# A column plan ended 40 steps earlier, and 50 scatters spread over the steps behind it

## The chip, the cores and the metric

The kernel runs on one core of one Trainium2 chip. The metric is the device time of one execution in microseconds (us); the figure of a kernel is the median of its runs.

## The reference, cut to what matters

A graph network of four layers over N = 6250 nodes with D = 64 features and E = 206250 edges, sorted by destination. Each layer forms a message for each edge from its two ends and reduces the messages of a node to sum, sum of squares, greatest and least:

```python
msg = jnp.concatenate([h[src], h[dst]], axis=1) @ WM + bM
s = segment_sum(msg, dst); mean_sq = segment_sum(msg * msg, dst) / denom
mx = segment_max(msg, dst); mn = segment_min(msg, dst)
agg = jnp.concatenate([mean, mx, mn, std, var, s], axis=1)
hu = jnp.concatenate([h, agg, agg * amp, agg * att], axis=1) @ WU + bU
out = leaky_relu(batchnorm(hu / sqrt(n)) @ Wmix + bmix) + h
h = relu(batchnorm(out)) + h
```

In front stands a layer norm with a relu, and at the end the input x is added.

## The kernel before, in words

The nodes lie in 50 blocks of 125. Of a node's sources in one block, one is handled by a matmul with a one-hot operand; this covers the larger part of the edges. The sources left over are handled as "columns": rows of a table in device memory that are gathered one by one.

**The one-hot stage.** Each of the four layers has 13 chunks (NCH) of 482 destination nodes (CH), and each chunk goes through the 50 blocks (TILES). One block of one chunk is a *step*, so a layer has 13 x 50 = 650 steps, numbered 0 to 649 within the layer. In a step TensorE issues three matmuls (`products`, L1638) into one of five PSUM banks G and adds 1 to the semaphore `g_ready`; then it issues three more (`sums`, L1645) into a further bank. That makes six matmuls for a step. VectorE takes the running maximum of the bank (`greatest`, L1271; L1269 for the first two of a chunk) once `g_ready` says that it is full, and adds 1 to `g_used`; TensorE waits for `g_used` before it fills that bank again, so it can be five steps ahead of VectorE and no more. The one-hot operand is loaded by the SP queue (`fetch`, L448, one load for five steps, a ring of five) from `ohd`, which the first layer makes (`compare`, L1287, with loads of `vd`) and stores.

**The columns.** A plan made in Python (`COL_GROUPS`) holds 166 groups of one to three columns, 457 in all (STATIC). GpSimd gathers them (L808, one indirect DMA for each column, 128 rows) into a ring of five groups; a group may be gathered once `joined` says that the group five places ahead of it is done with and once `g_ready` has come to within 12 steps (AHEAD) of the step at which the group is due. VectorE works a group in at its due step and the two after it, with four instructions (L1324, L1325, L1328, L1333), between the running maxima. `COL_SPAN = (56, 580)` lays the due steps evenly over steps 56 to 580. Three steps after its end VectorE has a branch for columns past the plan, which no data of this case needs.

**The end row.** When the last group is joined, GpSimd writes the accumulators `accL` back to rows of `left` with 50 indirect DMAs (L836, 128 rows of 1 KB each, `RT` = 50), waits for all of them, and loads `left` in the order of nodes into `accL` with ten DMAs (L841). GpSimd executes its queue in order. The node part begins after step 649 (VectorE L1449 and what follows it) and needs the first two of these ten loads, then two more at every fifth of its 25 turns. In the last chunk ACT's queue also loads the results of the one-hot stage back (`load_dense`, L646) after the first 8, 24, 32 and 40 blocks, and SP's queue fetches on until half of that chunk.

`wait(eng, s, value)` waits for a semaphore and, where the value depends on the layer, adds 1 to a semaphore of its own.

Of the kernel before, what the change touches and what calls it, by code (L numbers as in the profile page):

```python
# [24 lines left out]
TILES = 50  # L25
# [26 lines left out]
NCH = 13  # L52
# [14 lines left out]
RT = TILES  # L67
# [40 lines left out]
COL_GROUPS = LEAD + [g for g in COL_GROUPS if g not in LEAD]  # L108
SLOT_COLS = [sum(w for _, _, w in COL_GROUPS[b::RING_G]) for b in range(RING_G)]

COL_SPAN = (56, 580)
AHEAD = 12

REST = RT * ROUND
BINS = ROUND + 4
# [36 lines left out]
def build(nc, x, src, dst, WM, bM, WU, bU, gamma_t, beta_t, Wmix, bmix, gamma_o, beta_o, out):  # L152
# [14 lines left out]
    with ExitStack() as ctx:  # L167
# [188 lines left out]
        def wait(eng, s, value):  # L356

            wait_at(eng, s, value)
            if not isinstance(value, int):
                eng.sem_inc(S["passed"])  # L360

        def wait_at(eng, s, value):

            eng.wait_ge(S[s] if isinstance(s, str) else s, value)
# [378 lines left out]
        def _(pool):  # L743
# [37 lines left out]
            with pool.Fori(0, LAYERS) as l:  # L781
# [16 lines left out]
                NG = len(COL_GROUPS)  # L798
                first, last = COL_SPAN
                fetched = 0  # L800
                for g, (r, t, w) in enumerate(COL_GROUPS):
                    b = g % RING_G
                    fetched += w
                    wait(pool, "joined", l * NG + g + 1)
                    wait(pool, "g_ready", l * (NCH * TILES) + first + fetched * (last - first) // STATIC - AHEAD)
                    for k in range(w):
# [26 lines left out]
                    pool.sem_inc(S["passed"])  # L833

                for t in range(RT):
                    nc.gpsimd.indirect_dma_start(left, bass.IndirectOffsetOnAxis(ap=lists[:, t * PAY + D:t * PAY + D + 1], axis=0),  # L836
                                                 acc3[:, t, :], None).then_inc(S["lf_sc"], 16)
                wait(pool, "lf_sc", (l + 1) * (16 * RT))
# [6 lines left out]
        def _(dve):  # L845
# [391 lines left out]
            def dense_part(l, numbers, chunks):  # L1237
# [97 lines left out]
                def columns_at(first, last):  # L1335


                    done, due = 0, {}
                    for g, (_, _, w) in enumerate(COL_GROUPS):
                        done += w  # L1340
                        k = first + done * (last - first) // STATIC
                        for part in range(3):
                            due.setdefault(k + part, []).append((g, part))
                    return due
# [38 lines left out]

                dense(0 if numbers else l * (NCH * TILES), COL_SPAN)

# [165 lines left out]
        def _(pe):  # L1551
# [56 lines left out]
            def layer(l, stored):  # L1608
# [74 lines left out]
                def columns(j):  # L1683

                    i = l * HALF + j
                    q = j % 2
                    for g, (j0, _, _) in enumerate(M_GROUPS):
                        if j == j0:
                            wait(pe, m_ld[g], l * 32 + 32)
                    if j >= 2:  # L1690
                        wait(pe, "t_used", i - 1)
                    for k, v in enumerate((MT, ST)):
                        for a in range(2):
                            nc.tensor.transpose(TPS[q][0:NP, (2 * k + a) * P:(2 * k + a + 1) * P],  # L1694
                                                v[:, (2 * j + a) * NP:(2 * j + a + 1) * NP], ident[:, :])
                    if j >= 1:
                        wait(pe, "t_used", i)
                    nc.tensor.matmul(BPS[0:NP, 0:P], hT[:, j * NP:(j + 1) * NP], W[:, W_BB:W_BB + P],  # L1698
                                     start=True, stop=True).then_inc(S["t_ps"], 1)
# [92 lines left out]
```

## Time and profile before

| | |
|---|---|
| time, median of 3 runs | 4816.18 us (4803.33 to 4818.72) |
| span of the profiled execution | 4821.6 us |
| TensorE busy with matmuls | 3895.8 us, 81% |
| VectorE busy | 3426.7 us, 71% |
| GpSimd busy | 2229.1 us, 46% |
| 200 scatters (L836) | 195.6 us |
| 1828 gathers (L808) | 1832.8 us |

The span reaches from the first to the last instruction of one execution; it is 5.4 us (0.1%) above the median of the runs. Busy times of the engines overlap each other. "Idle before" is the time in which an engine did nothing just before an instruction of the group; the name behind it is what ended the idle time by the semaphore events, and "remote" means that no instruction on record could be named for it.

### The profile page before, as it was taken

What the parts mean: (1) busy time and instruction counts of PE and PEld (TensorE: products, weight loads), DVE (VectorE), ACT (ScalarE), POOL (GpSimd) and SP (SyncE); (2) the same over time, 40 slices, a digit from 0 to 9 for tenths busy, and PEclk for the clock granted to TensorE, in tenths of its full rate; (3) what the DMA queues carried; (4) which work ended last, traced back from release to release, by engine and by line L of the source; (5) the groups of instructions that cost most, each with busy time, mean ns of one, the idle gap of its engine ahead of it and who ended that gap; (6) DMA issues with size and microseconds to landing.
All of it is one profiled execution on the core that took longest, in us unless ns stands there. A gap on an engine that the chain in (4) does not pass through costs nothing.

```text
span 4821.6 us, 69713 instructions
## 1 busy us (share of the span) xinstructions
PE 3895.8 (81%) x19240; PEld 2004.6 (42%) x19240; DVE 3426.7 (71%) x7809; ACT 508.7 (11%) x1496; POOL 2229.1 (46%) x2241
## 2 busy tenths in 40 slices
PE   0165999998688999999587999999597999899586
PEld 0022444443265444444265444444265444444255
DVE  5795888898477777777377777777367677777466
ACT  4211000000034000000034000000024000000024
POOL 6204566666500566666500556666500466666600
PEclk9987999999799999999799999999799999999898
DMA  6005888888741444444531444444441444444450
GB/s 176 9 16 146 223 228 217 229 234 212 208 155 58 139 137 136 139 136 136 155 117 55 136 132 127 146 135 131 140 151 40 130 137 140 134 136 131 133 171 28
DMA packets 302954, 667.77 MB, mean 138 GB/s; under 512 B 82191, under 2 KB 180677, under 8 KB 302435
## 3 DMA queue, kind: packets, MB, share of 16 engines
q1 hardware_dynamic: 188676, 419.32, 29.7%
q0 software_dynamic: 81280, 191.65, 15.3%
q10 hardware_dynamic: 32732, 54.15, 3.4%
q14 instruction: 208, 1.70, 0.1%
q8 instruction: 58, 0.95, 0.1%
HBM read 517.17 MB, written 151.72 MB: 139 GB/s over the span
## 4 chain that ended last, share of the span: by engine, by line
PE 58%; another core or an unknown queue 19%; DVE 10%; issue 6%; ACT 2%; POOL 2%; DMA 1%; ACTq 1%; DVEq 0%; SPq 0%; POOLq 0%
PE bank L1638 27%; PE bank L1645 24%; PE bank L1722 3%; DVE scr L1271 2%; POOL accL L766 1%; PE bank L1710 1%; DVE RE L1082 1%; POOL accL L758 1%; DVE accL L1038 1%; DMA RE<-vd 1%; DVE accL L1039 1%; PE bank L1620 1%; PE bank L1694 0%; ACT scr L690 0%
## 5 line engine op out<-in xcount | busy, mean ns | idle before, releaser
L808 POOL DMA_INDIRECT rows<-table,lists x1828 | 1832.8, 1003 | 1269.8 <-issue 645.0
L1638 PE MATMUL bank<-RE,split 126*128 126x482 bf16 x7800 | 2061.8, 374 | 346.5 <-DVE scr L1271 268.4
L1271 DVE TENSOR_TENSOR scr<-scr,bank 128x482 f32<-128x482 f32 x2496 | 1594.6, 649 | 1026.5 <-PE bank L1638 615.0
L1645 PE MATMUL bank<-RE,split 125*128 125x482 bf16 x7800 | 2058.5, 373 | 143.1 <-ACT scr L565 122.7
L1638 PEld LDWEIGHTS bank<-RE,split 126*128 126x128 bf16 x7800 | 749.8, 98 | 1272.9 <-DVE scr L1271 348.5
L1645 PEld LDWEIGHTS bank<-RE,split 125*128 125x128 bf16 x7800 | 766.8, 98 | 1016.1 <-ACT scr L565 128.9
L565 ACT COPY scr<-bank 128x482 f32<-128x482 f32 x52 | 29.1, 560 | 3704.9 <-PE bank L1645 1772.1
L1333 DVE TENSOR_TENSOR accL<-accL,rows 128x384 f32<-128x384 f32 (+2 forms) x664 | 342.8, 516 | 0.0
L1328 DVE SCALAR_TENSOR_TENSOR rows<-CNT,rows 128x384 f32<-128x384 f32 (+2 forms) x664 | 342.6, 516 | 0.0
L793 POOL MEMSET accL<- 128x3328 f32 x4 | 11.5, 2871 | 682.5 <-DVE split L1260 681.5
L836 POOL DMA_INDIRECT left<-accL,lists x200 | 195.6, 978 | 110.5 <-issue 110.5
L1324 DVE TENSOR_TENSOR accL<-accL,rows 128x192 f32<-128x192 f32 (+2 forms) x664 | 221.0, 333 | 1.7 <-issue 1.0
L1325 DVE TENSOR_TENSOR accL<-accL,rows 128x192 f32<-128x192 f32 (+2 forms) x664 | 220.7, 332 | 0.0
L1722 PE MATMUL bank<-W,rows 128*125 128x192 f32 x624 | 126.5, 340 | 39.8 <-ACT scr L690 39.8
L772 POOL DMA_INDIRECT pos_d<-accL,nid x50 | 50.1, 1002 | 230.5 <-DVE nid L1163 215.5
L1287 DVE TENSOR_SCALAR RE<-RE,col 126x2410 bf16<-126x2410 bf16 x130 | 113.2, 871 | 28.2 <-DMA RE<-vd 26.5
L1722 PE MATMUL bank<-W,RE 128*125 128x192 f32 x576 | 113.1, 332 | 20.2 <-ACT scr L690 19.3
L1722 PEld LDWEIGHTS bank<-W,rows 128*125 128x125 f32 x624 | 101.8, 193 | 47.9 <-issue 38.1
L1269 DVE COPY scr<-bank 128x482 f32<-128x482 f32 x104 | 67.0, 655 | 59.3 <-remote 28.4
L1722 PEld LDWEIGHTS bank<-W,RE 128*125 128x125 f32 x576 | 90.7, 187 | 28.0 <-issue 25.1
L1449 DVE TENSOR_TENSOR rows<-bank,accL 125x256 f32<-125x256 f32 x100 | 42.6, 426 | 77.8 <-PE bank L1698 76.1
L1710 PE MATMUL bank<-ident,aggb 125*128 125x125 f32 x600 | 83.4, 276 | 4.8 <-DVE aggb L1469 4.8
(272 smaller groups left out, 2370.6 us busy)
## 6 DMA issues: line engine op xcount, KB each, us to landing
RE<-ohd SPq DMA_DIRECT2D x395, 593.1 KB
RE<-vd SPq DMA_DIRECT2D x130, 593.1 KB
ohd<-RE SPq DMA_DIRECT2D x130, 593.1 KB
rows<-table,lists POOLq DMA_INDIRECT x1828
dense_d<-scr ACTq DMA_DIRECT2D x104, 241.0 KB
accL<-left POOLq DMA_DIRECT2D x40, 625.0 KB, 19.3
split<-dense_d ACTq DMA_DIRECT2D x16, 750.0 KB, 8.6
table<-accL SPq DMA_DIRECT2D x36, 250.0 KB
```

Of the source, the lines that this page charges most:

```text
L808: nc.gpsimd.indirect_dma_start(ring[:, b * GC + k, :], None, table, bass.IndirectOffsetOnAxis(ap=lists[:, c:c + 1], axis=0)).then_inc(col_ ...
L836: nc.gpsimd.indirect_dma_start(left, bass.IndirectOffsetOnAxis(ap=lists[:, t * PAY + D:t * PAY + D + 1], axis=0), acc3[:, t, :], None).the ...
L1271: nc.vector.tensor_tensor(accM[k % 2], accM[k % 2], G[k % RING][:, 0:CH], ALU.max).then_inc(S["g_used"], 1)
L1287: nc.vector.tensor_scalar(BK[b][0:NP + 1, :], VB[g % 2][0:NP + 1, :], answers[0:NP + 1, :], None, ALU.is_equal).then_inc(S["cmp"], 1)
L1324: nc.vector.tensor_tensor(acc[:, :, 2 * D:3 * D], acc[:, :, 2 * D:3 * D], got[:, :, 0:D], ALU.max)
L1325: nc.vector.tensor_tensor(acc[:, :, 3 * D:4 * D], acc[:, :, 3 * D:4 * D], got[:, :, 0:D], ALU.min).then_inc(S["tops"], 1)
L1328: nc.vector.scalar_tensor_tensor(got, bcast(CNT[:, t:t + w].unsqueeze(2), [P, w, 2 * D]), float(r), got, ALU.is_gt, ALU.mult).then_inc(S[" ...
L1333: nc.vector.tensor_tensor(acc[:, :, 0:2 * D], acc[:, :, 0:2 * D], got, ALU.add).then_inc(S["joined"], 1)
L1638: ins = nc.tensor.matmul(G[k % RING][:, 0:CH], split[0:NP + 1, ORDER[k], q, 0:2 * D], columns_of(k, NP + 1), start=q == 0, stop=q == 2)
L1645: ins = nc.tensor.matmul(SB[:, 0:CH], split[0:NP, ORDER[k], q, D:3 * D], columns_of(k, NP), start=k == 0 and q == 0, stop=k == TILES - 1 a ...
L1710: ins = nc.tensor.transpose(FPS[(2 * j + a) % 3][:, c * NP:(c + 1) * NP], agg[j % 2][0:NP, a, 2 * c:2 * c + 2, :], id125)
L1722: nc.tensor.matmul(u, aggT[j % 2][a][:, c * NP:(c + 1) * NP], W[:, W_U + c * 192:W_U + (c + 1) * 192], start=a == 0 and c == 0, stop=False ...
```

## The change

The plan of the columns spans steps 56 to 540, 40 steps fewer than before, with the same 457 columns in the same order. The 50 scatters of the end row each get a wait of their own on `g_ready`: the scatter of number t waits for step 546 + 3 t // 2 of the layer, thus 546, 547, 549, 550, 552 and so on to 619. Nothing else differs; VectorE's branch for columns past the plan moves with the end of the span, from step 583 to 543.

```diff
-COL_SPAN = (56, 580)
+COL_SPAN = (56, 540)
 AHEAD = 12
+SCATTER_AT = [COL_SPAN[1] + 6 + 3 * t // 2 for t in range(RT)]
...
                 for t in range(RT):
+                    wait(pool, "g_ready", l * (NCH * TILES) + SCATTER_AT[t])
                     nc.gpsimd.indirect_dma_start(left, bass.IndirectOffsetOnAxis(ap=lists[:, t * PAY + D:t * PAY + D + 1], axis=0),
                                                  acc3[:, t, :], None).then_inc(S["lf_sc"], 16)
                 wait(pool, "lf_sc", (l + 1) * (16 * RT))
```

## Rows read from the trace of the kernel before

**Rows 1.** The page's first line.

```profile
span 4821.6 us, 69713 instructions
```

**Rows 2.** The page's groups: busy us, mean ns of one | idle before, its releaser.

```profile
L808 POOL DMA_INDIRECT rows<-table,lists x1828 | 1832.8, 1003 | 1269.8 <-issue 645.0
...
L1271 DVE TENSOR_TENSOR scr<-scr,bank 128x482 f32<-128x482 f32 x2496 | 1594.6, 649 | 1026.5 <-PE bank L1638 615.0
...
L836 POOL DMA_INDIRECT left<-accL,lists x200 | 195.6, 978 | 110.5 <-issue 110.5
```

**Rows 3.** Windows, second layer: steps 10 to 44, steps 620 to 649.

```profile
core 0: us, PE busy (x) PEld busy (x) DVE busy (x) ACT busy (x) POOL busy (x), PEclk, DMA share, GB/s
1538.37:1579.98 41.61, 41.61 (x205) 19.75 (x204) 36.40 (x73) 0.00 (x0) 0.00 (x0) 1.00 0.46 150
...
2416.54:2452.03 35.49, 35.49 (x176) 16.85 (x175) 19.04 (x30) 0.00 (x0) 0.00 (x0) 1.00 0.77 242
```

**Rows 4.** Windows, steps 56 to 580: first layer, fourth layer, sum of all four.

```profile
503.45:1226.37 722.92, 667.76 (x3146) 304.20 (x3145) 617.44 (x1296) 6.62 (x11) 472.19 (x450) 0.97 0.86 224
...
3781.49:4506.61 725.12, 666.28 (x3146) 304.74 (x3144) 539.50 (x1190) 5.60 (x10) 444.99 (x450) 0.97 0.47 136
sum 2896.67, PE 2664.64 PEld 1220.04 DVE 2240.06 ACT 24.18 POOL 1805.10; mean PE 666.16 PEld 305.01 DVE 560.02 ACT 6.04 POOL 451.28
```

**Rows 5.** Windows, steps 584 to 649: first, second, fourth layer, sum of four.

```profile
1231.26:1378.20 146.94, 88.23 (x392) 39.26 (x391) 52.01 (x83) 0.56 (x1) 55.04 (x60) 0.78 0.73 225
2318.18:2452.03 133.85, 85.48 (x392) 38.39 (x391) 42.93 (x67) 0.56 (x1) 53.95 (x60) 0.80 0.62 186
...
4511.51:4646.77 135.26, 84.63 (x391) 38.34 (x390) 44.45 (x71) 0.56 (x1) 53.98 (x60) 0.79 0.60 184
sum 549.82, PE 344.04 PEld 154.43 DVE 182.37 ACT 2.24 POOL 216.94; mean PE 86.01 PEld 38.61 DVE 45.59 ACT 0.56 POOL 54.24
```

**Rows 6.** Windows inside two bursts of indirect DMAs, and behind the second.

```profile
386.48:446.19 59.71, 20.09 (x60) 6.99 (x61) 10.44 (x19) 8.76 (x18) 44.90 (x44) 0.59 0.45 132
...
2319.00:2340.00 21.00, 18.03 (x87) 8.14 (x85) 6.31 (x10) 0.00 (x0) 15.70 (x17) 1.00 0.47 153
2340.00:2384.00 44.00, 5.36 (x12) 1.30 (x12) 1.97 (x3) 0.00 (x0) 32.98 (x34) 0.51 0.34 118
...
2400.00:2440.00 40.00, 40.00 (x198) 18.98 (x197) 21.55 (x33) 0.00 (x0) 0.00 (x0) 1.00 0.95 272
```

**Rows 7.** Timeline of VectorE in that burst: start, us, instruction, idle before.

```profile
2326.42 0.66 DVE L1271 TENSOR_TENSOR scr<-scr,bank 128x482 f32<-128x482 f32 x1 [0.57 <-DVE scr L1271]
...
2355.49 0.66 DVE L1271 TENSOR_TENSOR scr<-scr,bank 128x482 f32<-128x482 f32 x1 [12.68 <-remote]
2371.59 0.66 DVE L1271 TENSOR_TENSOR scr<-scr,bank 128x482 f32<-128x482 f32 x1 [15.45 <-remote]
```

**Rows 8.** Timeline of GpSimd, second layer: the first scatter, the loads behind the last.

```profile
2319.42 1.00 POOL L836 DMA_INDIRECT left<-accL,lists  x1 [10.89 <-issue]
...
2385.08 5.26 POOL L841 DMA_DIRECT2D accL<-left  x10 [2.04 <-DMA left<-accL,lists]
```

**Rows 9.** Timelines of VectorE and GpSimd in the column stage.

```profile
1937.06 0.66 DVE L1271 TENSOR_TENSOR scr<-scr,bank 128x482 f32<-128x482 f32 x1 [5.08 <-PE bank L1638]
...
1935.42 0.94 POOL L808 DMA_INDIRECT rows<-table,lists  x1 [0.30 <-issue]
1941.53 0.94 POOL L808 DMA_INDIRECT rows<-table,lists  x1 [5.17 <-PE bank L1638]
```

**Rows 10.** Windows in the column stage, from a gather's start to another's.

```profile
2033.00:2157.90 124.90, 113.11 (x540) 51.81 (x539) 91.61 (x201) 1.12 (x2) 76.37 (x79) 0.99 0.48 137
...
2856.50:2881.00 24.50, 17.73 (x80) 7.67 (x79) 13.80 (x30) 0.00 (x0) 14.59 (x15) 0.85 0.38 112
2900.50:2918.40 17.90, 16.23 (x79) 7.36 (x78) 12.65 (x28) 0.00 (x0) 12.13 (x12) 1.00 0.40 117
```

**Rows 11.** The page's DMA issues: count, KB each, median us to landing.

```profile
accL<-left POOLq DMA_DIRECT2D x40, 625.0 KB, 19.3
```

## The prediction

> **What bounds the kernel now.** I read the page first. In its span [rows 1] TensorE is the busiest engine, and the costliest groups are the two matmul lines of the one-hot stage, the gathers and VectorE's running maximum. The scatters are a small group, 195.6 us for 200 [rows 2]; on the page they look like nothing. So I cut each layer into windows and asked what a step costs in each.
>
> An undisturbed step is the yardstick. Steps 10 to 44 of the second layer, before any gather, take 41.61 us for 34 steps, and steps 620 to 649 take 35.49 us for 29 [rows 3]. Both give 1.224 us for a step, with TensorE busy throughout. At this rate TensorE is the bound.
>
> Steps 56 to 580 carry the columns. They are 524 steps and would take 524 x 1.224 = 641.3 us; the four layers take 2896.67 us together, 724.2 each [rows 4]. The excess is 331.6 us in all, 82.9 for a layer.
>
> Steps 584 to 649 carry the scatters and the loads. They are 65 steps and would take 79.5 us, 318.2 for four layers; they take 549.8 [rows 5]. The excess is **231.6 us**, 4.8% of the time, and it is not spread out: the last 29 of these steps run at the yardstick [rows 3].
>
> The burst itself tells why. GpSimd starts scatter 1 at 2319.42 and the loads at 2385.08 [rows 8], and 2.04 us of the time between them is a wait: the 50 scatters take 63.6 us, 1.27 us each, of which 0.98 is busy [rows 2] and 0.3 a gap. In the first 21 us TensorE still issues 87 matmuls, nearly its full pace; in the next 44 us it issues 12, and the granted clock is 0.51, the lower of the two levels, after an engine that had been almost idle [rows 6]. The DMA engines are no explanation: their share is 0.34 there, and it is 0.95 in the window behind, where TensorE never pauses [rows 6]. VectorE's maximum still lasts 0.66 us but is preceded by 12.68 and 15.45 us of idleness [rows 7], although its bank's matmuls were issued long before. What comes late is the notice that a bank is full. TensorE then has no free bank and stops too. The same picture, 60 matmuls in 59.7 us, stands at the very start of the first layer, where another burst of 44 indirect DMAs runs [rows 6]; the change doesn't touch that one.
>
> The column stage shows a mild form. VectorE waits 5.08 us for TensorE's notice, and it gets it at 1937.06, just after GpSimd's row of gathers ended at 1936.4; GpSimd's own pause is 5.17 us, because it waits for the same count [rows 9]. There the disturbance ends itself: gathers hang on `g_ready`, so when notices stop, gathers stop, and the notices come through. The scatters of before hang on nothing and go on for 63.6 us.
>
> **The change part by part.**
>
> *The scatters.* From 546 to 619 there are 73 steps for 50 scatters: 73 x 1.224 / 49 = 1.82 us from one to the next, where the burst had 1.27. GpSimd's idle time between two grows from 0.3 to about 0.85 us on average. And each now waits for the count, which makes the disturbance end itself as in the column stage. What the 50 can still cost: below, nothing; above, what a gather costs, 82.9 / 450 = 0.18 us each, 9 us for a layer. Gathers come 1.6 us apart on average but in rows without a pause, the scatters never in such rows, so I take 1 us for a layer. The 50 waits and their increments on GpSimd cost its queue time in which it would be idle anyway; without that cover they would move the loads, which are not urgent (below). Behind the scatters in GpSimd's queue stand only the wait for their landing and the ten loads.
>
> *The loads.* The last scatter leaves at step 619, and the loads some 3 us later [rows 8], about 35 us before the stage's end instead of 67 us. They are 10 x 625 KB = 6.25 MB [rows 11], which takes 23 us at the 272 GB/s of rows 6, but it shares that rate with the other two queues. The first pair, all that the node part needs at its start, is at the front of its queue; the median load lands after 19.3 us [rows 11]. Its cover is thus 35 us against about 20. The later pairs have a fifth of the node part each. The row of ten issues takes 5.26 us without a pause [rows 8], in which notices may be late; TensorE can be five steps, 6.1 us, ahead. Bounds 0 and 5.3 us for a layer; I take 2.
>
> So the scatter part gives -231.6 + 4 x (1 + 2) = **-220 us**, bounds -232 and 4 x (9 + 5.3) - 232 = -174.
>
> *The columns.* The same 457 gathers and 166 groups lie in 484 steps: a gather each 1.059 steps, 1.30 us at the yardstick, where it was 1.147 steps or 1.40 us. GpSimd needs 1.25 us at least (0.94 and 0.30 [rows 9]). It had 10% to spare and now has 4%, so rows of gathers without a pause, which are what delays the notices, get longer. VectorE has room: 560 us busy of 724 [rows 4]; 40 maxima fewer at 0.65 us take 26 us off, so it is busy 534 us of a stage of about 700. In the first layer it is busy 617 us of 723, and would be 591 of 700; tight, but below. What limits the stage is then how fast gathers can go through the cycle of a long row and a pause. In before this is 724.2 / 450 = 1.61 us a gather over the whole stage, with rows that are short because the schedule isn't due yet. In the stretches of long rows it is 79 in 124.9 us (1.58), 12 in 17.9 us (1.49) and, at worst, 15 in 24.5 us (1.63) [rows 10]. I take 1.55, between best and worst: 450 x 1.55 = 697.5 us for steps 56 to 540, and then 40 steps at the yardstick, 49.0 us, are in the place of steps 540 to 580. That is 746.5 against 724.2, **+22.3 us for a layer, +89 in all**. Bounds: 1.49 gives 719.5 (-19 in all), 1.63 gives 782.5 (+233). A stage of 697.5 us for 484 steps is 1.44 us a step, 0.22 above the yardstick, where before it was 0.16 above.
>
> *The branch* for columns past the plan moves from step 583 to 543 and costs the same there.
>
> Sum: -220 + 89 = -131 us. Against the profiled span of 4821.6 that is 4691, against the median of the runs, 5.4 lower, **4685 us** (-2.7%).
>
> **Rivals.**
>
> 1. *The columns cost nothing.* Each gather keeps its excess of 0.18 us, however dense. Then only the 220 us count: 4596. For it: windows with more gathers don't look slower in steps; 12 in 17.9 us come with 79 matmuls, 1.36 us a step [rows 10]. Chance 0.09.
> 2. *The gathers keep their pace of 1.61 us.* If what delays notices works like a cap on the rate of indirect DMAs, the column stage takes its 724 us for 484 steps too, and the 40 freed steps come on top: +49 us a layer, +196. Then 4816 - 220 + 196 = 4792. For it: the four layers are alike within 1% although the first has 224 GB/s of DMA traffic and the last 136 [rows 4]. Against it: 1.49 us occurs. Chance 0.17. If it gets as bad as 1.63 everywhere the sum is +13 and the time 4829, the same as before within what can be told; 0.03.
> 3. *The loads come too late.* In the last 35 us of the stage the DMA engines move 9.5 MB at 272 GB/s; the ten loads, ACT's loads of results and the last fetches want more. If the first pair comes 15 us after the stage's end in each layer: 4685 + 60 = 4745. Against it: the pair is first in its queue. The Trainium skill, in "DMA: Bandwidth & Descriptors", section "Queues, rings and completion order", says that a DMA engine takes turns between the queues that have work, by packets; by that the loads would get at least a third of the rate, so the pair's 1.25 MB would be there in about 14 us. No row of before shows that split. Chance 0.06.
> 4. *The price is for each scatter, not for the row of them* (the other side). Divided up, the burst costs 231.6 / 200 = 1.16 us a scatter, about what one keeps GpSimd busy (0.978 us [rows 2]). If every scatter stops VectorE while it is issued, spacing gives nothing back, and the columns' price stays: 4816 + 89 = 4905. It decides as soon as more than 0.6 of that price stays with each spaced scatter. The Trainium skill, in "SBUF — State Buffer", section "Who interferes with whom", has a rule that points this way: VectorE and GpSimd share a pair of ports under an exclusive lock, the loser blocks for the whole instruction. It adds that an instruction with one operand in SBUF doesn't take part, and the maximum has one there and one in PSUM. By that lock each of 50 scatters would cost 0.97 us, near the 1.16. The rows speak against it: the first 17 scatters let 87 matmuls through and the next 34 only 12 [rows 6], the maximum isn't longer in the burst [rows 2, 7], and 450 gathers as long as a scatter cost 0.18 us each. Chance 0.05.
> 5. *The change doesn't do what it says*: GpSimd comes to the end row so late that the steps waited for are past and the scatters leave in a row again. The last group is due at 540 and the first scatter at 546, and a late GpSimd holds up the due steps too; chance 0.02, with a time near 4905.
>
> **How the numbers follow.** The likeliest case, scatters cured and columns dearer by -5 to +40 us a layer, has 0.58 and a range of its own of 4596 to 4755. A measurement of this kernel tells about 0.3%, 14 us, from no change. Faster: 0.58 + 0.09 + 0.17 + 0.06 = 0.90. Same: 0.03. Slower: 0.05 + 0.02 = 0.07. The range goes from the price-free columns to just short of rival 2, whose upper half stays out with the slower cases: 4595 to 4785.
>
> **What would show it.** In the changed profile: steps 584 to 649 in 80 to 85 us instead of 134 to 147, with TensorE's granted clock at 1.00 there; scatters with two distances, about 1.3 and 2.4 us, and idle time that ends with TensorE; no wait of VectorE over some 5 us outside the start of the first layer; the loads about 35 us before the node part and no wait of the first VectorE instruction of the node part for them. Steps 56 to 540 in about 698 us: 675 would be rival 1, 724 rival 2. The forecast is wrong if TensorE's pauses in steps 546 to 619 add up to more than 15 us a layer, or if the column stage is outside 670 to 735 us.

## The result, and the profile after

The changed kernel takes **4860.24 us** in the median of 4 runs (4852.42 to 4875.11), the kernel before 4817.45 in its 4 (4803.33 to 4822.94). The ratio is 1.0084, with a 95% interval of 1.0054 to 1.0115. So it is slower by 0.8%, a small loss, but the interval does not reach 1, where I had forecast 4685 us and a chance of 0.90 for faster. The profiled execution after has a span of 4852.7 us, 31.1 more than [rows 1], and that is the difference to explain.

The page of the changed kernel, its groups in the form of [rows 2]:

```profile
span 4852.7 us, 70113 instructions
...
L809 POOL DMA_INDIRECT rows<-table,lists x1828 | 1815.5, 993 | 1319.7 <-issue 656.4
...
L1273 DVE TENSOR_TENSOR scr<-scr,bank 128x482 f32<-128x482 f32 x2496 | 1608.0, 652 | 1048.4 <-PE bank L1640 583.1
...
L838 POOL DMA_INDIRECT left<-accL,lists x200 | 199.3, 997 | 216.6 <-PE bank L1640 168.7
```

Lines have moved: L808 is now L809, L836 is L838, L1271 is L1273, L1638 is L1640. The scatters (L838) did what was meant: GpSimd is idle for 216.6 us ahead of them instead of 110.5, and 168.7 us of that end with TensorE's count. Nothing else on the page shows where the time went, so the windows must.

Windows of the changed kernel, steps 584 to 649 in the four layers and their sum, to hold against [rows 5]:

```profile
1292.36:1403.63 111.27, 85.10 (x391) 38.97 (x390) 49.44 (x78) 0.56 (x1) 31.97 (x35) 0.86 0.89 269
2409.95:2489.50 79.55, 79.55 (x391) 37.75 (x390) 43.27 (x67) 0.56 (x1) 28.66 (x35) 1.00 0.79 229
3503.40:3582.95 79.55, 79.55 (x392) 37.75 (x391) 43.28 (x67) 0.56 (x1) 28.66 (x35) 1.00 0.79 228
4599.18:4678.73 79.55, 79.55 (x391) 37.75 (x390) 43.27 (x67) 0.56 (x1) 28.68 (x35) 1.00 0.80 224
sum 349.92, PE 323.75 PEld 152.22 DVE 179.26 ACT 2.25 POOL 117.97; mean PE 80.94 PEld 38.05 DVE 44.82 ACT 0.56 POOL 29.49
```

Three layers run at exactly the yardstick of 1.224 us for a step, with TensorE busy throughout and its granted clock at 1.00. The first layer has 31.7 us too many. In all 349.9 us stand where 549.8 stood: **-199.9 us**, where I forecast -220.

Windows of the changed kernel, steps 56 to 540, which now carry the whole plan (second and fourth layer, sum of all four), and then steps 56 to 580, the stretch of [rows 4] (fourth layer, sum):

```profile
1620.24:2356.11 735.87, 638.22 (x2906) 286.17 (x2904) 516.39 (x1150) 5.79 (x10) 441.17 (x450) 0.93 0.45 127
...
3813.06:4545.34 732.28, 642.15 (x2906) 286.15 (x2905) 515.45 (x1148) 5.04 (x9) 439.70 (x450) 0.93 0.44 128
sum 2930.61, PE 2560.36 PEld 1142.92 DVE 2136.66 ACT 22.36 POOL 1786.77; mean PE 640.09 PEld 285.73 DVE 534.16 ACT 5.59 POOL 446.69
...
3813.06:4594.29 781.23, 691.10 (x3146) 309.39 (x3144) 546.52 (x1202) 5.60 (x10) 461.97 (x473) 0.93 0.45 130
sum 3126.43, PE 2756.18 PEld 1235.77 DVE 2264.11 ACT 24.61 POOL 1877.74; mean PE 689.05 PEld 308.94 DVE 566.03 ACT 6.15 POOL 469.44
```

The plan takes 2930.6 / 4 = 732.7 us for 484 steps. Before it took 724.2 us for 524. The steps have become fewer and the time has not: 450 gathers in 732.7 us are 1.63 us each, after 1.61. Over the same steps 56 to 580 the sum grows from 2896.7 to 3126.4: **+229.8 us**, where I forecast +89. The two stretches give -199.9 + 229.8 = +29.9, and the span has grown by 31.1. All else together moved by 1.2 us.

Of the 140 us a layer that the plan's steps take over the yardstick (732.7 against 592.4), TensorE is idle for 92.6; the rest are the same matmuls taking longer, 640.1 us busy, at a granted clock of 0.93. Without the gathers (experiment 8 below) they are busy for 592.7 us at 1.00. So about a third of the loss is paid in the clock that falls with the pauses.

What a bad moment of the column stage looks like after, in the timeline of GpSimd and then of VectorE (second layer; start, us, instruction, idle time ahead and its releaser), and the window over it:

```profile
2112.16 0.94 POOL L809 DMA_INDIRECT rows<-table,lists  x1 [0.30 <-PE bank L1640]
...
2128.96 0.94 POOL L809 DMA_INDIRECT rows<-table,lists  x1 [0.30 <-issue]
2135.38 0.98 POOL L809 DMA_INDIRECT rows<-table,lists  x1 [5.47 <-DVE accL L1335]
```

```profile
2125.24 0.66 DVE L1273 TENSOR_TENSOR scr<-scr,bank 128x482 f32<-128x482 f32 x1 [3.10 <-PE bank L1640]
...
2132.28 0.66 DVE L1273 TENSOR_TENSOR scr<-scr,bank 128x482 f32<-128x482 f32 x1 [5.84 <-remote]
```

```profile
2122.00:2133.00 11.00, 4.07 (x21) 1.58 (x18) 2.05 (x6) 0.00 (x0) 6.08 (x7) 0.77 0.35 101
```

It is the cycle of [rows 9] again. GpSimd issues one gather each 1.25 to 1.57 us without a pause until 2128.96; VectorE goes on at 2132.28, 2.4 us after that last gather has ended; TensorE is busy for 4.07 of the 11 us in between. That VectorE is late, and not TensorE, shows in TensorE's own timeline (three matmuls a line):

```profile
2119.61 0.78 PE L1640 MATMUL bank<-RE,split 126*128 126x482 bf16 x3
...
2125.96 0.78 PE L1640 MATMUL bank<-RE,split 126*128 126x482 bf16 x3 [1.29 <-issue]
...
2132.99 1.39 PE L1640 MATMUL bank<-RE,split 126*128 126x482 bf16 x3 [5.64 <-DVE scr L1273]
```

Counted off from the start of the execution, one filled bank to each maximum, the maximum at 2132.28 takes the bank that was filled from 2119.61 to 2120.39. Four more banks had been filled behind it, the last from 2125.96, and then TensorE had no free one. Counted in this way over the steps 56 to 540, VectorE stands idle with its next bank already full for 140 us in the first layer and 210 to 216 in each of the others (by the ends of matmuls that the trace models); in the kernel without gathers, experiment 8, it is 2 and 35 us. GpSimd's own pause is ended here by VectorE's join (L1335), because the ring of five groups is full. Over the whole kernel the waits of gathers for joins rise from 112.1 to 234.8 us, and those for TensorE's count fall from 427.6 to 360.2: GpSimd is now behind the plan so often that the plan holds it up less, and the ring more.

### The profile page after: what moved, and what is told of

It is laid out like the page before. It is cut to its first block, busy times and chain, and to the rows that moved or that the text cites. A ratio compares the mean times of both kernels' runs of the same rounds, so it can differ in the third digit from the quotient of the medians.

```text
span 4852.7 us, 70113 instructions
## 1 busy us (share of the span) xinstructions
PE 3965.6 (82%) x19240; PEld 2014.5 (42%) x19240; DVE 3439.9 (71%) x7809; ACT 509.0 (10%) x1496; POOL 2216.5 (46%) x2241
## 4 chain that ended last, share of the span: by engine, by line
PE 53%; another core or an unknown queue 18%; DVE 13%; issue 9%; ACT 2%; DMA 2%; POOL 1%; ACTq 1%; DVEq 0%; SPq 0%
PE bank L1640 25%; PE bank L1647 22%; PE bank L1724 3%; DVE scr L1273 2%; DMA RE<-vd 1%; PE bank L1712 1%; DVE rows L1330 1%; DVE RE L1084 1%; POOL accL L767 1%; POOL accL L759 1%; DVE accL L1040 1%; DVE accL L1041 1%; DVE accL L1335 1%; PE bank L1622 1%
## 5 line engine op out<-in xcount | busy, mean ns | idle before, releaser
L809 POOL DMA_INDIRECT rows<-table,lists x1828 | 1815.5, 993 | 1319.7 <-issue 656.4
L1640 PE MATMUL bank<-RE,split 126*128 126x482 bf16 x7800 | 2097.4, 379 | 384.5 <-DVE scr L1273 292.1
L1273 DVE TENSOR_TENSOR scr<-scr,bank 128x482 f32<-128x482 f32 x2496 | 1608.0, 652 | 1048.4 <-PE bank L1640 583.1
L1647 PE MATMUL bank<-RE,split 125*128 125x482 bf16 x7800 | 2092.3, 378 | 64.0 <-ACT scr L566 37.3
L1640 PEld LDWEIGHTS bank<-RE,split 126*128 126x128 bf16 x7800 | 754.2, 99 | 1351.5 <-DVE scr L1273 389.8
L1335 DVE TENSOR_TENSOR accL<-accL,rows 128x384 f32<-128x384 f32 (+2 forms) x664 | 344.2, 518 | 0.0
L838 POOL DMA_INDIRECT left<-accL,lists x200 | 199.3, 997 | 216.6 <-PE bank L1640 168.7
L794 POOL MEMSET accL<- 128x3328 f32 x4 | 11.5, 2870 | 600.7 <-DVE split L1262 599.7
L773 POOL DMA_INDIRECT pos_d<-accL,nid x50 | 50.7, 1015 | 230.9 <-DVE nid L1165 216.0
L1271 DVE COPY scr<-bank 128x482 f32<-128x482 f32 x104 | 66.5, 656 | 30.0 <-PE bank L1640 12.5
```

Source lines behind the costliest of these rows:

```text
L809: nc.gpsimd.indirect_dma_start(ring[:, b * GC + k, :], None, table, bass.IndirectOffsetOnAxis(ap=lists[:, c:c + 1], axis=0)).then_inc(col_ ...
L1273: nc.vector.tensor_tensor(accM[k % 2], accM[k % 2], G[k % RING][:, 0:CH], ALU.max).then_inc(S["g_used"], 1)
L1335: nc.vector.tensor_tensor(acc[:, :, 0:2 * D], acc[:, :, 0:2 * D], got, ALU.add).then_inc(S["joined"], 1)
L1640: ins = nc.tensor.matmul(G[k % RING][:, 0:CH], split[0:NP + 1, ORDER[k], q, 0:2 * D], columns_of(k, NP + 1), start=q == 0, stop=q == 2)
L1647: ins = nc.tensor.matmul(SB[:, 0:CH], split[0:NP, ORDER[k], q, D:3 * D], columns_of(k, NP), start=k == 0 and q == 0, stop=k == TILES - 1 a ...
```

## The experiments

The kernel before took 4824.15 us in the median of 7 runs beside experiments 1 to 4, 4824.4 (one run) beside 5 to 8, and 4821.75 (7 runs) beside 9 to 12. Experiments 4, 5 to 8 and 12 have one run each; they are read by their windows.

### 1. The scatters' waits alone

```diff
 COL_SPAN = (56, 580)
+SCATTER_AT = [586 + t for t in range(RT)]
...
                 for t in range(RT):
+                    wait(pool, "g_ready", l * (NCH * TILES) + SCATTER_AT[t])
```

> The columns stay on steps 56 to 580; only the scatters get waits, scatter t for step 586 + t, so 586 to 635. Before, the scatters' steps 584 to 620 had an excess of 231.6 us over the yardstick of 1.224 us a step, in the changed kernel 0 us. If unbroken rows of indirect DMAs are what delays the notices, and the pace of the rows is limited to one in about 1.6 us (theory CAP), 50 scatters one step apart take 50 x 1.6 = 80 us where 49 steps take 60: an excess of about 20 us a layer, so 231.6 - 80 = 150 us less than before, about 4665. If what matters is only that the scatters hang on the count (theory SELF-ENDING), the excess is under 8 us a layer and the time about 4610, plus what the loads behind step 635, 17 us before the node part, hold that up. The column stage should take its 724 us a layer again by both.

It took 4635.41 us (4631.70 to 4646.80), ratio 0.9609 (0.9570 to 0.9649): **-189 us**. Steps 56 to 580 sum to 2891.70, as before. Windows of this kernel, steps 584 to 649, second layer and sum of four:

```profile
2281.79:2369.70 87.91, 82.25 (x392) 37.83 (x391) 40.80 (x67) 0.56 (x1) 53.93 (x60) 0.98 0.67 218
...
sum 352.25, PE 329.56 PEld 151.30 DVE 175.26 ACT 2.24 POOL 219.66; mean PE 82.39 PEld 37.83 DVE 43.81 ACT 0.56 POOL 54.91
```

The sum of [rows 5] was 549.8. The excess over 318.2 is now 34.1 us, 8.5 for a layer, with the 50 scatters 1.46 us apart in the second layer. In the changed kernel they are 1.82 us apart and the excess of the three undisturbed layers is nil. Spacing cures the burst, and how far depends on the distance. The time lies between what the two theories gave, 4665 for a limit of 1.6 us on scatters too and 4610 for none: scatters that each wait for a step went faster than the gathers ever did, at a small price. Of the gain in the windows, 12.3 us are paid back behind the stage, where VectorE waits for the loads.

### 2. The shorter plan alone

```diff
-COL_SPAN = (56, 580)
+COL_SPAN = (56, 540)
```

> The columns are put on steps 56 to 540 and the scatters get no waits: the other half of the change alone. CAP: the gathers keep their 1.60 to 1.63 us each, steps 56 to 540 take about 733 us a layer as in the changed kernel, +230 us over before for steps 56 to 580, and the burst of scatters costs about its 54 to 67 us a layer again, at step 546: about 5045. If the columns' excess came from something that the waiting scatters do (they are behind all gathers in the queue, so this is unlikely), steps 56 to 540 would take less than 700 us.

It took 5057.18 us (5052.59 to 5066.10), ratio 1.0485 (1.0443 to 1.0526): **+233 us**. Its steps 56 to 540 sum to 2943.88, 736.0 for a layer. The bursts of scatters are back in the 109 steps behind, which take 187.9 us on average and would take 133.4. The two halves add up: -189 + 233 = +44, and the whole change measured +43. That they do so this well is partly luck: experiment 1 still pays 34.1 us for its scatters and 12.3 for the loads, and the whole change pays 31.7 in the first layer's tail in their place. The sign is plain all the same. The shorter plan is the loss.

### 3. A wait for each gather

Before, the wait stands ahead of a group of up to three gathers. Here each gather has its own:

```diff
...
-                    wait(pool, "g_ready", ... + first + fetched * (last - first) // STATIC - AHEAD)
                     for k in range(w):
+                        wait(pool, "g_ready", ... + first + (fetched - w + k + 1) * (last - first) // STATIC - AHEAD)
```

> As before, but each gather waits for its own share of the schedule, 1.147 steps after the one ahead of it, where a group of up to three waited once and left in a row. If the price comes from the length of unbroken rows (theory ROWS), the rows are gone at the yardstick's pace (1.40 us from gather to gather against 1.25 needed), and the column stage's excess of 83 us a layer falls by at least a third: 4700 or less. If it is a limit on the mean pace of indirect DMAs, 1.6 us each (CAP), nothing changes within 20 us a layer: 4740 to 4900.

It took 4919.76 us (4913.97 to 4931.34), ratio 1.0200 (1.0158 to 1.0242). Steps 56 to 580, sum: 2995.03, which is 98 us more than [rows 4]. The stage takes 748.8 us a layer and the gathers come 1.66 us apart, slower than both theories had it (4700 or less, and 4740 to 4900). It does not test row length, though: I had expected the rows to be gone, and they are not. Gathers that follow each other without a pause come in rows of 5.4 on average, where the kernel before has 6.6, and rows of ten or more still hold a third of all gathers, where it was 43%. GpSimd is behind the schedule, so most of the new waits are over before it comes to them. What the length of the rows is worth stays open.

### 4. The plan over steps 56 to 640

```diff
-COL_SPAN = (56, 580)
+COL_SPAN = (56, 640)
```

> The columns are laid over steps 56 to 640, the scatters behind them without waits: read only the column stage; the scatters and loads now stand in the way of the node part, which makes the whole slower. A gather is due each 1.278 steps, 1.564 us at the yardstick. CAP: 457 gathers at 1.6 us take 731 us; steps 56 to 640 take 584 x 1.224 = 715 us without excess, so an excess of only 10 to 30 us a layer, and the pace of the gathers is 1.6 to 1.62 us for the third time. If each gather costs 0.18 us however dense (the first rival of the prediction), the excess stays at 83 us.

One run: 4581.21 us. The stage runs almost at the yardstick. The scatters now leave at the very end of the stage and behind it, and the node part waits for their rows. Timelines of this kernel, the loads on GpSimd and the first instruction of the node part on VectorE:

```profile
2341.40 3.72 POOL L841 DMA_DIRECT2D accL<-left  x7 [2.06 <-DMA left<-accL,lists]
```

```profile
2349.99 0.43 DVE L1449 TENSOR_TENSOR rows<-bank,accL 125x256 f32<-125x256 f32 x1 [66.38 <-DMA accL<-left]
```

The wait of 66.38 us is what the node part pays for a plan that ends late, and the kernel is still 5% faster. It is timed again as experiment 9.

### 5 to 8. What in a gather sets the pace

If the pace of 1.6 us is a limit, what is it a limit of? Four edits of the changed kernel, all with the plan over 56 to 540, each take one thing away. Three of them (5, 6 and 8) also clear the gathers' buffer once, ahead of the first layer, since part of it is no longer filled. Half the rows of each gather:

```diff
-  nc.gpsimd.indirect_dma_start(ring[:, b * GC + k, :], None, table, bass.IndirectOffsetOnAxis(ap=lists[:, c:c + 1], axis=0))
+  nc.gpsimd.indirect_dma_start(ring[0:64, b * GC + k, :], None, table, bass.IndirectOffsetOnAxis(ap=lists[0:64, c:c + 1], axis=0))
```

> The changed kernel, but each gather fetches 64 rows in place of 128 (it leaves out the other half of the rows; the accumulations go on with what stands in the buffer). Read only steps 56 to 540, 733 us a layer in the changed kernel with an excess of 140 over the yardstick. If the limit of 1.6 us a gather is made of descriptors or bytes (theory TRAFFIC), the excess falls at least by half: 592 to 660 us. If it is a price of each DMA instruction whatever it carries (theory INSTRUCTION), it stays at 720 to 740.

Half the bytes of each row (`ring[:, b * GC + k, 0:D]` from a table seen as half rows, so that it also reads other rows of the table):

> The changed kernel, but each of the 128 rows of a gather brings 256 bytes in place of 512 (it leaves out the squares). It parts the two halves of TRAFFIC: if bytes set the pace, steps 56 to 540 take 592 to 660 us a layer; if the number of descriptors does, or the instruction, they stay at 715 to 740.

The four column instructions of VectorE on one element instead of up to 3 x 128, for example:

```diff
-  nc.vector.tensor_tensor(acc[:, :, 0:2 * D], acc[:, :, 0:2 * D], got, ALU.add).then_inc(S["joined"], 1)
+  nc.vector.tensor_tensor(acc[:, :, 0:1], acc[:, :, 0:1], got[:, :, 0:1], ALU.add).then_inc(S["joined"], 1)
```

> The changed kernel, but the four column instructions of VectorE work on one element of each row (it leaves out nearly all accumulation), while all gathers and semaphores stay. If indirect DMAs alone set the pace (CAP), steps 56 to 540 stay above 700 us a layer, since a VectorE with time to spare can't make notices come sooner. If the pace comes from a VectorE that can't catch up after a late notice (theory CATCH-UP), the excess of 140 us falls at least by half, to 592 to 660 us.

And no gathers at all in the stage, with every instruction of VectorE left at its size:

```diff
-                    for k in range(w):
-                        ...
-                        nc.gpsimd.indirect_dma_start(ring[:, b * GC + k, :], ...).then_inc(col_g[b], 16)
...
-                        wait_at(dve, col_g[b], ...)
```

> The changed kernel without the gathers (it leaves them out, and VectorE's wait for them; VectorE's column work and GpSimd's waits stay). CAP: no indirect DMA, no late notice: steps 56 to 540 at 592 to 600 us a layer. If VectorE's denser work were the bound by itself, they would stay above 650.

They took 4898.30, 4854.54, 4825.54 and 4303.05 us. Windows of each, steps 56 to 540, sum of the four layers; for experiment 8 the second layer too. Half the rows:

```profile
sum 2965.24, PE 2557.91 PEld 1145.01 DVE 2133.01 ACT 21.84 POOL 1693.35; mean PE 639.48 PEld 286.25 DVE 533.25 ACT 5.46 POOL 423.34
```

Half the bytes:

```profile
sum 2927.72, PE 2559.80 PEld 1147.94 DVE 2136.75 ACT 21.87 POOL 1791.78; mean PE 639.95 PEld 286.98 DVE 534.19 ACT 5.47 POOL 447.94
```

Small work of VectorE:

```profile
sum 2899.61, PE 2533.66 PEld 1137.59 DVE 1469.86 ACT 22.00 POOL 1727.56; mean PE 633.41 PEld 284.40 DVE 367.46 ACT 5.50 POOL 431.89
```

No gathers:

```profile
1481.76:2074.08 592.32, 592.32 (x2906) 281.11 (x2905) 544.31 (x1153) 5.80 (x10) 0.00 (x0) 1.00 0.35 108
...
sum 2370.62, PE 2370.62 PEld 1124.77 DVE 2221.58 ACT 21.78 POOL 0.00; mean PE 592.65 PEld 281.19 DVE 555.40 ACT 5.44 POOL 0.00
```

The changed kernel has 2930.61 there. Half the rows and half the bytes change nothing for the better (+35 and -3 us). A third of VectorE's load taken away (2136.66 to 1469.86 us busy) gives back 31 us, 8 for a layer, of an excess of 140. Without the gathers the whole excess is gone: 592.3 us for 484 steps is the yardstick, to the digit, with VectorE just as busy. So the stage is held up by the gathers' being issued, hardly by what one moves (64 rows in place of 128 and half the bytes change it by +1.2% and -0.1%) and little by what VectorE does with it. A VectorE that waits for gathered rows is no rival: in the changed kernel it waits 0.4 us for them in the whole execution.

### 9 to 12. Where the plan should lie

Experiment 9 is experiment 4, timed. Experiment 10 starts the plan earlier, ends it at 616, and gives the first 28 scatters a step each and the rest the last one:

```diff
-COL_SPAN = (56, 540)
+COL_SPAN = (32, 616)
-SCATTER_AT = [COL_SPAN[1] + 6 + 3 * t // 2 for t in range(RT)]
+SCATTER_AT = [min(622 + t, NCH * TILES) for t in range(RT)]
```

Experiment 11 is the kernel before with `COL_SPAN = (32, 640)`. Experiment 12 is the changed kernel with the ten loads in pairs, each pair behind a step of its own, to see whether their burst causes the first layer's loss:

```diff
                 for g in range(5):
+                    wait(pool, "g_ready", l * (NCH * TILES) + 622 + 6 * g)
                     for a in range(2):
                         nc.gpsimd.dma_start(Lv...
```

> The kernel of the run with columns on steps 56 to 640 and no waits at the scatters, now timed in rounds: 4581 again, 5% under the kernel before. CAP: its column stage is nearly free of excess since the gathers are due 1.56 us apart, and what it pays is about 66 us a layer in which the node part waits for scatters and loads.

> The version that CAP suggests: GpSimd's chain of 457 gathers at 1.6 us, 50 scatters and the loads is what a layer can't be shorter than, so start it earlier. Columns on steps 32 to 616, so the gathers start at step 20 in place of 44, and scatter t waits for step 622 + t, at most 650. From the stage's start: 24 us + 731 us of gathers + 8 us until the last is joined + 50 x 1.43 us + 6 us + 9 us for the first load = about 850 us to the first instruction of the node part, where the kernel with columns to 640 takes 880: 120 us less in four layers, about 4460. If what limits gathers were the steps and not the time, it would be no faster than 4560.

> Columns on steps 32 to 640, scatters without waits. The gathers are due 1.33 steps, 1.63 us, apart: above CAP's limit, so the column stage should have no excess at all (under 8 us a layer). The chain: 24 + 744 + 18 + 64 + 3 + 9 = 862 us, 18 a layer less than with 56 to 640: about 4510.

> The changed kernel, but its ten loads wait in pairs for steps 622, 628, 634, 640 and 646. The changed kernel lost 32 us between steps 620 and 649 of the first layer alone, where VectorE waits 25 us for a load of SP's queue that only that layer has (vd, 593 KB). If the ten loads crowd it out (theory CROWDING), the loss falls under 12 us, and the other layers stay as they are: about 4838. If that load is late for another reason, the loss stays at about 30 us. The column stage is untouched: 733 us.

Experiment 9: 4578.67 us (4574.82 to 4588.39), ratio 0.9496 (0.9452 to 0.9540). Experiment 10: **4498.74 us** (4489.77 to 4509.41), ratio 0.9332 (0.9289 to 0.9375), the best version of the study, 6.7% under the kernel before and 7.4% under the changed one. Experiment 11: 4552.23 us (4548.40 to 4556.14), ratio 0.9438 (0.9395 to 0.9480). Experiment 12, one run: 4865.68. Experiments 10 and 11 came 39 and 42 us above what I had expected (4460 and 4510). The stages took what was expected of them, and in the second to fourth layer of experiment 10 the node part starts 854 to 856 us into the layer (expected 850); but the kernel that I reckoned from, experiment 9, needs 871 to 876 there and not 880, and the first layers are longer, 906 us in experiment 10.

Windows over the plan's steps, second layer and sum of four. Experiment 9, steps 56 to 640:

```profile
1539.43:2261.83 722.40, 717.55 (x3506) 339.07 (x3505) 591.64 (x1255) 6.94 (x12) 453.25 (x450) 1.00 0.51 152
...
sum 2900.00, PE 2870.71 PEld 1354.29 DVE 2431.03 ACT 26.70 POOL 1841.28; mean PE 717.68 PEld 338.57 DVE 607.76 ACT 6.68 POOL 460.32
```

Experiment 10, steps 32 to 616:

```profile
1478.21:2205.67 727.46, 718.28 (x3505) 338.50 (x3504) 590.63 (x1272) 12.43 (x15) 452.87 (x450) 1.00 0.51 149
...
sum 2916.04, PE 2873.35 PEld 1354.37 DVE 2447.98 ACT 49.73 POOL 1841.56; mean PE 718.34 PEld 338.59 DVE 612.00 ACT 12.43 POOL 460.39
```

Experiment 11, steps 32 to 640:

```profile
1504.55:2249.80 745.25, 744.41 (x3650) 352.96 (x3649) 622.31 (x1296) 12.45 (x15) 456.55 (x451) 1.00 0.52 152
...
sum 2986.24, PE 2978.32 PEld 1411.28 DVE 2554.35 ACT 49.80 POOL 1856.53; mean PE 744.58 PEld 352.82 DVE 638.59 ACT 12.45 POOL 464.13
```

Put in one table, with the steps at 1.224 us, the due distance as that over 457 columns, the stage as a quarter of the windows' sum, and its distance as the stage over 450 gathers. The two distances have different divisors: over 450, the due 1.56 would read 1.59. So near it the excess says more than the distances do.

| plan, kernel | steps at the yardstick | due distance | stage, us | us a gather | excess, us a layer |
|---|---|---|---|---|---|
| 56 to 540, changed | 592.4 | 1.30 | 732.7 | 1.63 | 140 |
| 56 to 580, before | 641.3 | 1.40 | 724.2 | 1.61 | 83 |
| 56 to 640, exp. 9 | 714.8 | 1.56 | 725.0 | 1.61 | 10 |
| 32 to 616, exp. 10 | 714.8 | 1.56 | 729.0 | 1.62 | 14 |
| 32 to 640, exp. 11 | 744.2 | 1.63 | 746.6 | 1.66 | 2 |

In these five the stage takes 724 to 733 us wherever the plan asks for gathers denser than 1.6 us, and what the steps take where it asks for fewer. Among the others, experiments 2, 5 and 12 have 736.0, 741.3 and 735.7, experiment 7 has 724.9, and experiment 3, with a wait for each gather, has 748.8 for a plan that asks for 1.40. So the limit depends on the waits, and may depend on the ring and the banks, which were not varied. Experiment 10 beats 9 and 11 because it also gets the scatters and loads away sooner: VectorE waits for the loads for 161.0 us in the whole kernel, 40 a layer, against 268.2 in experiment 9 and 267.5 in 11. Here are GpSimd's first scatter and its loads in experiment 10, second layer:

```profile
2213.41 1.00 POOL L838 DMA_INDIRECT left<-accL,lists  x1 [16.78 <-PE bank L1640]
...
2284.48 5.26 POOL L843 DMA_DIRECT2D accL<-left  x10 [3.63 <-issue]
```

The 16.78 us ahead of the first scatter look like room for an earlier first step, but they aren't: VectorE joins the last group at 2209.59, and in experiment 4, where no scatter waits for a step, GpSimd is idle for 16.32 us at this place. About 2 us a layer could be gained.

Experiment 10 also shows that a short row of scatters is nearly free. In its second layer 23 of them leave ahead of step 649, 1.46 us apart, and steps 620 to 649 take 35.91 us where the yardstick has 35.49; the 50 of experiment 1, as dense, cost 8.5 us a layer.

Experiment 12's windows, steps 620 to 649, first and second layer:

```profile
1341.48:1406.16 64.68, 39.27 (x175) 17.63 (x174) 22.04 (x36) 0.00 (x0) 5.76 (x11) 0.79 0.85 247
2460.77:2496.26 35.49, 35.49 (x175) 16.85 (x174) 19.05 (x30) 0.00 (x0) 5.46 (x11) 1.00 0.97 256
```

The first layer still loses 64.68 - 35.49 = 29.2 us, where the changed kernel loses 31.7. My expectation had put under 12 us for crowding by the loads, so by its own terms this run speaks against that theory. It shows that ten issues in a row are not the cause. It does not clear the loads themselves: four of the ten (2.5 MB) have left when VectorE begins to wait at 1356.4, and two more leave at 1358.7. In the other three layers neither form costs anything.

## Why the prediction was wrong

**The scatters: right.** The burst was the whole of the 231.6 us, and 1.82 us between scatters takes it away entirely in three layers. Steps 546 to 619 of the second layer, window of the changed kernel:

```profile
2363.45:2452.79 89.34, 89.34 (x440) 42.40 (x439) 49.11 (x76) 1.12 (x2) 47.44 (x49) 1.00 0.62 195
```

73 steps at 1.224 us are 89.3, so the 50 scatters cost nothing (I had 1 us a layer) and the loads behind them nothing in three layers (I had 2). Rival 4, a price for each scatter, falls with it, and with it the port lock of the Trainium skill ("SBUF — State Buffer", "Who interferes with whom") as an explanation of this burst. The exception that the page makes, for an instruction of VectorE with at most one input in SBUF (outside its two-port modes), fits these rows.

**The first layer's tail: 31.7 us that I didn't have.** I asked whether the loads would come too late for the node part (rival 3). They didn't; they came at a bad moment for another queue. Windows of the changed kernel in the first layer, steps 620 to 649 and then the 30 us in which it happens; behind them VectorE's waits, and the DMA queues of those 30 us:

```profile
1336.41:1403.63 67.22, 41.05 (x175) 18.06 (x174) 22.79 (x37) 0.00 (x0) 5.42 (x11) 0.77 0.86 251
...
1344.00:1374.00 30.00, 13.38 (x66) 6.16 (x64) 4.71 (x8) 0.00 (x0) 3.30 (x7) 0.77 1.02 275
```

```profile
1376.41 0.85 DVE L1289 TENSOR_SCALAR RE<-RE,col 126x2410 bf16<-126x2410 bf16 x1 [25.06 <-DMA RE<-vd]
1391.28 0.85 DVE L1289 TENSOR_SCALAR RE<-RE,col 126x2410 bf16<-126x2410 bf16 x1 [11.19 <-DMA RE<-vd]
```

```profile
DMA packets 2399, 8.24 MB, mean 275 GB/s; under 512 B 213, under 2 KB 1022, under 8 KB 2397
...
q0 software_dynamic: 808, 3.56, 44.8%
q10 hardware_dynamic: 574, 3.07, 37.2%
q1 hardware_dynamic: 1015, 1.59, 20.1%
```

In the first layer SP's queue (q1) still fetches a block of the one-hot operand (RE<-vd, 593 KB) for each of VectorE's blocks. GpSimd's loads (q0) and ACT's loads of results (q10) fill the engines, share 1.02. q1 has the most packets, 1015 of 2399, and the fewest bytes, 1.59 of 8.24 MB. VectorE waits 25.06 and 11.19 us for its blocks, and TensorE stops behind it. The Trainium skill ("DMA: Bandwidth & Descriptors", "Queues, rings and completion order") says that an engine takes turns between its queues by packets. By that the queue with the small packets gets the smallest part of the bytes. The trace agrees in the order of the bytes; the packets are not shared out evenly (808, 574 and 1015). That this sharing is what made the fetch late is argued, not shown. I had used this rule in the prediction, and only for the side that gains by it.

How much steps 620 to 649 of the first layer lose goes with where the loads leave, in us from the start of step 620:

| kernel | loads leave at | excess, us |
|---|---|---|
| exp. 2 | -83 | 0.0 |
| before | -41 | 0.0 |
| exp. 3 | -20 | 18.2 |
| changed | +6 | 31.7 |
| exp. 5, 6, 7 | +5 to +6 | 33.8, 29.2, 30.9 |
| exp. 8, no gathers | +8 | 33.3 |
| exp. 12, in pairs | +6 | 29.2 |
| exp. 1 | +34 | 4.3 |
| exp. 10 | +73 | 1.2 |
| exp. 4, 9, 11 | +104 to +110 | 4.8, 11.5, 7.5 |

So it is not the early start by itself, since with loads that leave 41 us or more ahead of step 620 nothing is lost there; the loss goes with loads that fall close to it. The gathers have no part in it (experiment 8). In the last line the loads leave after the stage has ended, so a part of up to 11.5 us has another cause. How the loss divides between GpSimd's loads and ACT's wasn't tried.

**The columns: the step that failed.** It is the term "I take 1.55, between best and worst: 450 x 1.55 = 697.5 us". The mechanism, a pace that the gathers keep, stood in the text as rival 2, *the gathers keep their pace*, with a chance of 0.17; the runs showed it at the upper end, to which I had given 0.03. The pace measured is 1.63 us, the stage 732.7 us, and the sum +229.8 instead of +89. With it the prediction's own arithmetic gives +13 us (-220 + 233); with the first layer's 31.7 us in place of my allowance of 12 it gives about +33, and the profile has +31.1. The sign that I had set for this step was too wide to catch it: a stage outside 670 to 735 us, where 732.7 is enough to turn the gain into a loss.

Why I chose 1.55 is the useful part. The windows of [rows 10] hold whole rows of gathers with their pauses, but 12 or 15 gathers are too few. In the trace of before, any 12 gathers on end take from 1.26 to 2.28 us each, so 1.49 is no bound and 1.63 not the worst; any 79 take 1.50 to 1.71, and the long window's 1.58 is about the middle of that. From the first gather of a layer to its last it is 1.59 to 1.62. I took 1.55, below both the 1.58 over 79 gathers and the 1.61 of the whole stage. The stage as a whole, 1.61, I explained away: "rows that are short because the schedule isn't due yet". That could have been tested in before. The schedule asked for a gather each 1.40 us and got one each 1.61. A schedule that is asking faster than it is served cannot be what holds the gathers back. The pause of 5.17 us in [rows 9] is named for TensorE's count, but what delays the count is the gathers: without them (experiment 8) the steps run at the yardstick. Experiments 9 and 10 show it from the other side: with 1.56 us asked, next to nothing is lost, 10 and 14 us a layer.

The rest of the sum's setting held. VectorE's load, which I had called tight in the first layer, was not the bound: experiment 7 gives back 8 us a layer of 140, and experiment 8 leaves the load and loses the whole excess. Rival 1 (0.18 us a gather however dense) falls: the excess is 0.31 us a gather at 1.30 asked, 0.18 at 1.40, 0.02 at 1.56, none to speak of at 1.63.

**What stays open.** What in an indirect DMA makes VectorE go on late. It isn't rows or bytes, and VectorE's work is a small part of it. The prediction called it a late notice, but the rows show only that VectorE starts late on a bank that is long full; whether the notice is late or VectorE is late in taking up its next instruction, no run tells apart. Nor is it shown why gathers are held to 1.61 us while scatters with a wait each ran at 1.46 us for 8.5 us a layer, what the ring of five groups, the 12 steps (AHEAD) and the five banks have to do with the figure, or why experiment 3, with its finer waits, comes out slower.

## What to carry to other kernels

When a stream is slower than its own schedule asks for, take its measured pace over the whole stage for a limit and not for an average: price a denser schedule with that pace, and the steps that it frees at the full price of a step. Here one gather each 1.6 us goes by almost unseen beside a busy TensorE and a denser plan holds it up, so the 457 gathers belong over 584 steps or more; the count times the pace gives an estimate of the least length of the stage before anything is built. The figure has to be measured anew where waits, ring or banks differ. Fifty scatters beside a busy TensorE cost nothing at 1.8 us apart; after the stage, or in a short row at its end, they may be denser. And before transfers are moved, look at which other queue still feeds a critical wait in that stretch, and how small its packets are.

## What the runs showed of the hardware

- In this kernel a plan that asks for an indirect gather each 1.30 us gets one each 1.63, and TensorE and VectorE pause meanwhile, whatever the gathers move: 128 or 64 rows and whole or half rows give 732.7, 741.3 and 731.9 us for 450 of them. At 1.66 us (experiment 11) the matmuls run all but undisturbed, 2 us a layer over the yardstick.
- Fifty scatters 1.27 us apart beside the one-hot stage (before) went with a loss of 54 to 67 us a layer, 1.46 us apart (experiment 1) 7 to 11, and 1.82 us apart none. A row that ends soon costs little: with 23 scatters 1.46 us apart 0.4 us were lost in steps 620 to 649 of experiment 10's second layer.
- Without the gathers 484 steps take 592.3 us in three layers and 593.7 in the third, the granted clock is 1.00 and TensorE is busy for every microsecond. So the clock of 0.93 in the changed kernel's column stage comes with the pauses and is not what starts them; by the longer matmuls it adds 48 us a layer to their price.
- With the DMA engines full (share 1.02), a queue whose packets averaged 1.59 MB / 1015 = 1.6 KB moved 1.59 MB in 30 us, while one with 3.56 MB / 808 = 4.4 KB moved 3.56 MB.
